# A matmul engine's order in a fused recommender kernel: the third and fourth group of transposes moved within the steady batch tiles

## The chip, the cores and the metric

The kernel runs on one core of one Trainium2 chip. The metric is the device time of one execution in microseconds (us). The kernel before takes 982.83 us, the median of three runs (972.28, 982.83 and 982.91).

Names used below: PE is TensorE (matmuls and transposes), ACT is ScalarE, DVE is VectorE, POOL is GpSimd, SP is SyncE. PEld stands for PE's weight loads.

## The reference, cut to what matters

```python
cont_emb = emb_table[:13][None, :, :] * conts[:, :, None]     # 2048 x 13 x 64
cate_emb = emb_table[cates]                                   # 2048 x 26 x 64, gathered
cc = concatenate([cont_emb, cate_emb], axis=1)                # 2048 x 39 x 64
gram = einsum('bfd,bgd->bfg', cc, cc)
pairs = gram[:, ROWS, COLS]                                   # 741 products of each sample
X = concatenate([cont_emb.reshape(B, -1), cate_emb.reshape(B, -1), pairs], axis=1)
X = relu(_layernorm(X @ W1 + b1, ln1_g, ln1_b))               # 3237 -> 1024
X = relu(_layernorm(X @ W2 + b2, ln2_g, ln2_b))               # 1024 -> 1024
logit = sigmoid(X @ Wout + bout)
```

## The kernel before, in words

The batch of 2048 samples is cut into 16 tiles of 128 samples. A first stage computes, tile by tile, the first layer's 1024 columns and stores them to DRAM; a second stage (from about 755 us on) reads them back and does the second layer. The change concerns the first stage alone.

A tile x of the first stage has these parts:

- POOL gathers 26 embedding columns into `xb`, one indirect DMA each (L488), in four groups of 8, 6, 6 and 6 (`GROUPS`, two columns to a k-tile). It runs one tile ahead: the gathers of group g of tile x+1 wait until PE has transposed group g of tile x. Within a tile some gathers wait further, by `progress`: the one numbered 7 for `f_hi`, 10 for `late_hi`, 14 for `ts_hi` of all four groups, and 21, 23 and 25 for the dots taken from PSUM.
- PE transposes each group (L547; "next 0" is group 0 of the next tile, "own 1", "own 2", "own 3" are the second, third and fourth group). ACT rounds the result into `x_hl` (L766), DVE makes the low part (L1061), and both copy it to the layouts that the gram products want: ACT at L772 (`g_still`) and L777 (`g_move`), DVE at L1068.
- PE makes the pairwise products in four pieces, "gram 0" to "gram 3" (L590). "gram 0" needs the copies of all four groups. ACT and DVE take each piece out of PSUM (L807, L808, L1146, L1147); gram 2 and gram 3 wait until the pieces 0 and 1 are taken.
- From these DVE makes the features; PE transposes them in two steps, "factor" (L561) and "late" (L568, L569), and ACT and DVE split them (L789 and L1126 for factor, L794, L1132, L799 and L1138 for late).
- The first layer is 19 k-tiles of six matmuls each (L523, L524, L525): 0 to 12 are the embeddings, 13 to 18 the features. k-tiles 13 to 18 of a tile are done one iteration later, with "factor prev" and "late prev". k-tile 16 waits for `tail_lo`, the end of the late features' split (L1138). Behind k-tile 18 DVE and ACT do the layer norm of that tile (L1164 to L1192, L822).

Each engine has an order of its own, written out by hand. PE's is a tuple: `FIRST` for tile 0, `SECOND` for tile 1, `STEADY` for tiles 2 to 14 (thirteen iterations, of which twelve stand in a loop that holds two), `LAST` for tile 15. The file defines `STEADY` twice, and the second definition holds. ACT's and DVE's order stands in their functions `iteration`. For ACT it is, behind the factor's split of tile x: two `g_move` copies, the third group's split of tile x+1, the late features' hi part, a `g_move` copy, the tail's hi part, a `g_move` copy, the fourth group's split, and then the copies of the third and fourth group. DVE has the third group's low part ahead of the late features' low part as well.

Of the kernel before, what the change touches and what calls it, by code (L numbers as in the profile page):

```python
# [80 lines left out]
V_TILES = (CONT + 1) // 2  # L81
V_FIRST = (V_TILES - 1, 0, 1, 2)
V_BEHIND = {3: 3, 6: 4, 9: 5}
V_LAST = 5
IN_FLIGHT = 4


STEADY = (0, "own 1", 1, 2, 3, "factor prev", 4, "own 2", "late prev", 13, 14, "own 3", 5, 15, 16, 17, 18, 6, 7,
          "gram 0", 8, "gram 1", 9, "gram 2", 10, "gram 3", 11, "next 0", 12)
FIRST = (V_TILES - 1, 0, 1, 2)  # L90
V_BEHIND = {3: 3, 6: 4, 9: 5}
V_LAST = 5
IN_FLIGHT = 4


STEADY = (0, "own 1", 1, 2, 3, "factor prev", 4, "late prev", 13, 14, 5, "own 2", 15, 16, 17, "own 3", 18, 6, 7,
          "gram 0", 8, "gram 1", 9, "gram 2", 10, "gram 3", 11, "next 0", 12)
FIRST = (0, 1, 2, 3, "own 1", 4, 5, 6, "v 4", "own 2", 7, 8, "v 5", "own 3", 9, 10, "gram 0", "gram 1", 11,
         "gram 2", "gram 3", "next 0", 12)
# [42 lines left out]
def build(nc, conts, cates, emb, W1, b1, g1, be1, W2, b2, g2, be2, Wout, bout, rows, out):  # L142
    h1_dram = nc.dram_tensor("h1_scratch", (P, TILES, HID), F32, kind="Internal").ap()

    with ExitStack() as memory:
# [244 lines left out]
        def v_rows(n):  # L390

            m = min(P, CONT * DIM - n * P)
            return raw_hi[EK + n][0:m, :] if n < NF else h1_row[0:m, :]
# [3 lines left out]
        def _(sp):  # L397
# [5 lines left out]
            for k in range(EK):  # L403
                loads.append((raw_lo[k][:, :], (CONT + 2 * k) * DIM, w1_in[k]))
                if k in V_BEHIND:
                    n = V_BEHIND[k]
                    loads.append((v_rows(n), n * P, v_rows_in[n]))
# [3 lines left out]
            for n, (to, row, landed) in enumerate(loads):  # L411
                if n >= IN_FLIGHT:
                    sp.wait_ge(loads[n - IN_FLIGHT][2], 16)
                sp.dma_start(to, W1[row:row + to.shape[0], :]).then_inc(landed, 16)
# [105 lines left out]
        def _(pe):  # L520
# [81 lines left out]
            def v_product(n):  # L602
# [3 lines left out]
                for h in range(2):  # L606
                    done = nc.tensor.matmul(acc[1][0:CONT, h, :], vbd[0:rows_n.shape[0], n, :],
                                            rows_n[:, h * HALF:(h + 1) * HALF],
                                            start=n == V_FIRST[0], stop=n == V_LAST)
                if n == V_LAST:  # L610
                    done.then_inc(v_done, 1)
# [41 lines left out]

            def iteration(x, par, order=STEADY, first=False, last=False):

                if not isinstance(x, int) or x >= 2:
                    pe.wait_ge(norm_act, x - 1)
                    pe.wait_ge(norm_dve, x - 1)
                elif x == 1:
                    pe.wait_ge(v_in, 1)  # L660
                for what in order:
                    if isinstance(what, str):
                        share(x, what, first, last)
                    elif what < EK:
                        if first:
                            pe.wait_ge(w1_split, what + 1)
                        done = k_tile(x, par, what)
                        if last:
                            done.then_inc(w1_free, 1)
                    else:  # L670
                        if isinstance(x, int) and x == 1:
                            pe.wait_ge(w1_split, what + 1)
                        k_tile(x - 1, 1 - par, what)
                if last:
                    for kt in range(EK, KT):
                        if kt == EK + 2:
                            late(x)
                            transpose2(0, 0)
                        done = k_tile(x, par, kt)
                        if kt < KT - 1:  # L680
                            done.then_inc(w1_free, 1)
                    product2(0, 0, first=True)
# [45 lines left out]

            iteration(0, 0, FIRST, first=True)
            iteration(1, 1, SECOND)  # L730
# [658 lines left out]
```

## Time and profile before

| | us |
|---|---|
| three runs, median (lowest to highest) | 982.83 (972.28 to 982.91) |
| the profiled execution, its own time | 965.06 |
| its span, first to last instruction | 963.0 |
| PE busy in the span | 798.1 (83%) |
| DVE, ACT, POOL busy | 554.5, 500.7, 486.3 |
| mean granted clock of PE, share of full speed | 0.92 |

Times of the trace count from the span's start. Matmuls are pipelined, so a row that lasts 0.39 us may start 0.23 us behind the row ahead of it; the step between starts is what a matmul costs. A gram 0 starts at 345.24, 390.96, 434.76 and so on; from one gram 0 to the next is called a period below. Thirteen iterations follow the order `STEADY`, and each ends with a gram 0, the first at 162.19 and the last at 705.27.

### The profile page before, as it was taken

What the parts mean: (1) busy time and instruction counts of PE and PEld (TensorE: products, weight loads), DVE (VectorE), ACT (ScalarE), POOL (GpSimd) and SP (SyncE); (2) the same over time, 40 slices, a digit from 0 to 9 for tenths busy, and PEclk for the clock granted to TensorE, in tenths of its full rate; (3) what the DMA queues carried; (4) which work ended last, traced back from release to release, by engine and by line L of the source; (5) the groups of instructions that cost most, each with busy time, mean ns of one, the idle gap of its engine ahead of it and who ended that gap; (6) DMA issues with size and microseconds to landing.
All of it is one profiled execution on the core that took longest, in us unless ns stands there. A gap on an engine that the chain in (4) does not pass through costs nothing.

```text
span 963.0 us, 11843 instructions
## 1 busy us (share of the span) xinstructions
PE 798.1 (83%) x3583; PEld 630.0 (65%) x3583; DVE 554.5 (58%) x1704; ACT 500.7 (52%) x878; POOL 486.3 (51%) x451
## 2 busy tenths in 40 slices
PE   5386878888888778878788888888889899999995
PEld 1255666667666666657566666666667788888884
DVE  6255645454647273757455554646377765666668
ACT  2285745454646364565545544646468654444441
POOL 6776555555556455656555555556550013333331
PEclk9797979888999889998998989899999999999998
DMA  9998233222223232323232322323234621111100
GB/s 246 140 166 100 18 39 41 20 39 21 38 20 42 17 41 18 43 17 43 17 43 17 41 24 35 40 19 41 20 41 152 216 69 44 44 44 44 44 0 1
DMA packets 26232, 50.69 MB, mean 53 GB/s; under 512 B 10413, under 2 KB 10669, under 8 KB 26208
## 3 DMA queue, kind: packets, MB, share of 16 engines
q0 software_dynamic: 13344, 13.71, 21.6%
q1 hardware_dynamic: 10128, 27.97, 9.2%
q10 hardware_dynamic: 2736, 8.71, 2.3%
q8 instruction: 12, 0.20, 0.1%
q14 instruction: 12, 0.10, 0.0%
HBM read 41.96 MB, written 8.40 MB: 52 GB/s over the span
## 4 chain that ended last, share of the span: by engine, by line
PE 53%; ACT 14%; issue 14%; DVE 9%; DMA 7%; another core or an unknown queue 3%; SPq 0%; ACTq 0%; DVEq 0%
PE acc L523 15%; PE acc L525 14%; PE acc L524 14%; ACT g_move L777 6%; DMA raw_lo<-in_L_rec_W 5%; PE gr L590 3%; PE tr L590 2%; ACT g_still L772 2%; PE tr L547 2%; ACT x_hl L766 2%; DVE dots L1146 2%; DMA raw_hi<-in_L_rec_W 1%; DVE g_still L1068 1%; ACT dots L807 1%
## 5 line engine op out<-in xcount | busy, mean ns | idle before, releaser
L488 POOL DMA_INDIRECT xb<-in_L_rec_emb_table,idx x416 | 417.5, 1003 | 298.0 <-issue 141.6
L523 PE MATMUL acc<-w_hi,x_hl 128*128 128x512 f32 x416 | 183.8, 442 | 22.3 <-issue 15.3
L525 PE MATMUL acc<-w_hi,x_hl 128*128 128x512 f32 x416 | 174.6, 420 | 0.0
L524 PE MATMUL acc<-w_lo,x_hl 128*128 128x512 f32 x416 | 174.2, 419 | 0.0
L777 ACT CAST g_move<-x_hl 64x384 fp32r<-64x384 f32 (+1 forms) x192 | 125.5, 654 | 2.8
L507 POOL TENSOR_TENSOR raw_lo<-raw_lo,raw_hi 128x1024 f32<-128x1024 f32 x14 | 33.5, 2396 | 160.5 <-ACT raw_lo L946 160.5
L523 PEld LDWEIGHTS acc<-w_hi,x_hl 128*128 128x128 f32 x416 | 85.3, 205 | 43.5 <-issue 20.2
L523 PE MATMUL acc<-w_hi 128*128 128x512 f32 x256 | 101.3, 396 | 1.6 <-DVE w_lo L1339 1.6
L523 PE MATMUL acc<-w_hi,f_slots 128*128 128x512 f32 x192 | 85.3, 444 | 19.7 <-DVE f_slots L1138 12.9
L772 ACT CAST g_still<-x_hl 64x384 fp32r<-64x384 f32 (+1 forms) x96 | 99.0, 1032 | 1.9
L525 PE MATMUL acc<-w_hi,w_lo 128*128 128x512 f32 x256 | 100.0, 390 | 0.0
L524 PE MATMUL acc<-w_lo,w_hi 128*128 128x512 f32 x256 | 99.6, 389 | 0.0
L525 PEld LDWEIGHTS acc<-w_hi,x_hl 128*128 128x128 f32 x416 | 85.2, 205 | 20.3
L524 PEld LDWEIGHTS acc<-w_lo,x_hl 128*128 128x128 f32 x416 | 85.7, 206 | 14.2
L1061 DVE TENSOR_TENSOR x_hl<-tr,x_hl 128x512 fp32r<-128x512 f32 (+1 forms) x32 | 20.0, 625 | 123.0 <-ACT x_hl L766 116.5
L590 PE MATMUL gr<-g_move,g_still 128*128 128x124 f32 x256 | 40.8, 318 | 52.1 <-ACT g_move L777 37.5
L1061 DVE TENSOR_TENSOR x_hl<-gr,x_hl 128x384 fp32r<-128x384 f32 x32 | 17.8, 557 | 108.1 <-issue 81.3
L524 PE MATMUL acc<-w_lo,f_slots 128*128 128x512 f32 x192 | 79.1, 412 | 0.0
L525 PE MATMUL acc<-w_hi,f_slots 128*128 128x512 f32 x192 | 78.8, 410 | 0.0
L590 PEld LDWEIGHTS gr<-g_move,g_still 128*128 128x128 f32 x256 | 37.2, 220 | 62.6 <-ACT g_move L777 41.8
L766 ACT CAST x_hl<-gr 128x384 fp32r<-128x384 f32 x32 | 15.4, 480 | 117.6 <-remote 55.1
L1068 DVE TENSOR_SCALAR g_still<-x_hl 64x384 fp32r<-64x384 f32 (+1 forms) x96 | 66.6, 694 | 1.9
(117 smaller groups left out, 1280.0 us busy)
## 6 DMA issues: line engine op xcount, KB each, us to landing
raw_lo<-in_L_rec_W SPq DMA_DIRECT2D x26, 512.0 KB, 4.6
h_scratch<-h_row ACTq DMA_DIRECT2D x16, 512.0 KB
raw_hi<-h_scratch SPq DMA_DIRECT2D x16, 512.0 KB, 3.6
xb<-in_L_rec_emb_table,idx POOLq DMA_INDIRECT x416
raw_hi<-in_L_rec_W SPq DMA_DIRECT2D x6, 512.0 KB, 5.3
raw_hi<-in_L_rec_b SPq DMA_DIRECT2D x1, 512.0 KB, 4.3
raw_hi<-in_L_rec_ln_g SPq DMA_DIRECT2D x1, 512.0 KB, 5.2
raw_hi<-in_L_rec_ln_b SPq DMA_DIRECT2D x1, 512.0 KB, 6.0
```

The source lines that it names most:

```text
L488: nc.gpsimd.indirect_dma_start(out=xb[:, f * DIM:(f + 1) * DIM], out_offset=None, in_=emb, in_offset=bass.IndirectOffsetOnAxis(ap=idx[:, p ...
L507: nc.gpsimd.tensor_tensor(a2[par][:, :], n2[par][:, :], g2_bc, ALU.mult).then_inc(a2_mul, 1)
L523: nc.tensor.matmul(o, a, w, start=first, stop=False)
L524: nc.tensor.matmul(o, a, v, start=False, stop=False)
L525: return nc.tensor.matmul(o, b, w, start=False, stop=last)
L547: last = nc.tensor.transpose(t_bank(g)[:, (kt - a) * P:(kt - a + 1) * P], xb[:, kt * P:(kt + 1) * P], ident[:, :])
L590: last = nc.tensor.matmul(to, g_still[:, SAMPLES * j:SAMPLES * (j + 1), :].rearrange("p s f -> p (s f)"), g_move[:, :, j:P:P // SAMPLES], ...
L766: nc.scalar.copy(x_hl[:, 0, a:b, :].rearrange("p k b -> p (k b)"), t_bank(g)[:, 0:n]).then_inc(ts_hi, 1)
L772: nc.scalar.copy(*still_part(0, n, of))
L777: last = nc.scalar.copy(*move_part(n, m // 2, m % 2))
L1061: TT(x_hl[:, 1, a:b, :].rearrange("p k b -> p (k b)"), t_bank(g)[:, 0:n], x_hl[:, 0, a:b, :].rearrange("p k b -> p (k b)").bitcast(F32), A ...
L1068: last = TS(to, x_lo.bitcast(F32), 2.0, None, ALU.mult)
```

## The change

The second definition of `STEADY` is taken out, together with the repeated lines around it, so that the first one holds. It differs in two places: "own 2" stands behind k-tile 4 and ahead of "late prev" (it stood behind k-tile 5), and "own 3" stands behind k-tile 14 (it stood behind k-tile 17). `FIRST`, `SECOND` and `LAST` stay, and so do the orders of ACT, DVE, POOL and SP.

```diff
 STEADY = (0, "own 1", 1, 2, 3, "factor prev", 4, "own 2", "late prev", 13, 14, "own 3", 5, 15, 16, 17, 18, 6, 7,
           "gram 0", 8, "gram 1", 9, "gram 2", 10, "gram 3", 11, "next 0", 12)
-FIRST = (V_TILES - 1, 0, 1, 2)
-V_BEHIND = {3: 3, 6: 4, 9: 5}
-V_LAST = 5
-IN_FLIGHT = 4
-
-
-STEADY = (0, "own 1", 1, 2, 3, "factor prev", 4, "late prev", 13, 14, 5, "own 2", 15, 16, 17, "own 3", 18, 6, 7,
-          "gram 0", 8, "gram 1", 9, "gram 2", 10, "gram 3", 11, "next 0", 12)
```

PE before, from the end of k-tile 4 to the fourth group's transposes (`acc0` takes this tile's k-tiles, `acc1` those of the tile before; `f_slots` are features, `xb` the gathered embeddings):

```order
L525 MATMUL acc0<-w1_hi,x_hl 128x512
L568 MATMUL gr<-ident,dots 128x128 [waits chosen_done]
...
L569 MATMUL gr<-ident,feats 59x128
L523 MATMUL acc1<-w1_hi,f_slots 128x512 [waits f_lo]
...
L547 MATMUL tr<-ident,xb 128x128 [waits ts_lo,gathered2]
...
L523 MATMUL acc1<-w1_hi,f_slots 128x512 [waits tail_lo]
...
L547 MATMUL gr<-ident,xb 128x128 [waits ts_lo,gathered3]
```

The same stretch of PE now (line numbers are eight lower):

```order
L517 MATMUL acc0<-w1_hi,x_hl 128x512
L539 MATMUL tr<-ident,xb 128x128 [waits ts_lo,gathered2]
...
L560 MATMUL gr<-ident,dots 128x128 [waits chosen_done]
...
L561 MATMUL gr<-ident,feats 59x128
L515 MATMUL acc1<-w1_hi,f_slots 128x512 [waits f_lo]
...
L539 MATMUL gr<-ident,xb 128x128 [waits ts_lo,gathered3]
...
L515 MATMUL acc1<-w1_hi,f_slots 128x512 [waits tail_lo]
```

The third group's transposes (`gathered2`) now stand ahead of the late features' transposes, and the fourth group's (`gathered3`) ahead of the k-tile that waits for `tail_lo` instead of behind it. Between the fourth group's transposes and gram 0 there are now seven k-tiles (5, 15, 16, 17, 18, 6, 7), before there were three (18, 6, 7).

ACT's order over the same work, which is not changed (`x_hl<-tr` and `x_hl<-gr` are the splits of the third and the fourth group):

```order
L789 CAST f_slots<-tr 128x384 [waits f_trans]
L777 COPY g_move<-x_hl 64x7x128 x2
...
L766 CAST x_hl<-tr 128x384 [waits trans_ready]
L794 CAST f_slots<-gr 128x384 [waits l_trans]
L777 COPY g_move<-x_hl 64x7x128
L799 CAST f_slots<-gr 59x128 [waits late_lo]
L777 COPY g_move<-x_hl 64x7x128
...
L766 CAST x_hl<-gr 128x384 [waits trans_ready]
```

PE's order now names the third group, the late features and the fourth group in the sequence in which ACT waits for them; before, the late features came first.

## Rows read from the trace of the kernel before

**Rows 1.** Who PE waited for, 140 to 710 us: total us, times, longest us.

```profile
PE gr L590 <- ACT g_move L777: 36.2, 10, 3.7
PE tr L561 <- issue: 19.6, 6, 4.3
PE acc L523 <- DVE f_slots L1138: 12.9, 13, 1.0
PE gr L568 <- remote: 11.2, 5, 2.3
PE gr L590 <- issue: 11.0, 3, 3.7
PE gr L568 <- DVE dots L1154: 3.9, 3, 1.6
```

**Rows 2.** Windows by period: us, busy by engine (x rows), granted clock, DMA share, GB/s.

```profile
162.19:705.27 543.08, 442.99 (x1992) 352.10 (x1993) 298.19 (x1032) 286.40 (x468) 309.45 (x312) 0.91 0.28 31
345.24:390.96 45.72, 37.64 (x166) 30.14 (x167) 25.08 (x87) 24.17 (x39) 25.84 (x26) 0.90 0.27 30
390.96:434.76 43.80, 36.51 (x166) 28.84 (x167) 24.83 (x87) 23.74 (x39) 25.77 (x27) 0.90 0.29 31
705.27:738.48 33.21, 32.79 (x161) 26.92 (x161) 24.88 (x86) 23.95 (x39) 7.60 (x9) 0.95 0.31 74
```

**Rows 3.** Timeline of PE: start us, us, engine, line, operation, tiles, [idle before <-releaser].

```profile
370.74 0.55 PE L568 MATMUL gr<-ident,dots 128*128 128x128 f32 x3 [2.21 <-remote]
...
376.96 0.49 PE L547 MATMUL tr<-ident,xb 128*128 128x128 f32 x3
...
379.84 0.50 PE L523 MATMUL acc<-w_hi,f_slots 128*128 128x512 f32 x1 [0.99 <-DVE f_slots L1138]
...
382.69 0.49 PE L547 MATMUL gr<-ident,xb 128*128 128x128 f32 x3
...
390.96 1.11 PE L590 MATMUL gr<-g_move,g_still 128*128 128x124 f32 x8 [3.67 <-issue]
```

**Rows 4.** Timeline of ACT, the same stretch.

```profile
369.06 1.89 ACT L777 CAST g_move<-x_hl 64x896 fp32r<-64x896 f32 x2
...
377.48 0.48 ACT L766 CAST x_hl<-tr 128x384 fp32r<-128x384 f32 x1 [6.54 <-PE tr L547]
...
383.22 0.48 ACT L766 CAST x_hl<-gr 128x384 fp32r<-128x384 f32 x1 [2.79 <-issue]
...
388.47 2.07 ACT L777 CAST g_move<-x_hl 64x384 fp32r<-64x384 f32 x4
```

**Rows 5.** Timeline of PE in the last tile, which follows `LAST`.

```profile
726.42 0.49 PE L547 MATMUL tr<-ident,xb 128*128 128x128 f32 x3
...
729.96 0.49 PE L547 MATMUL gr<-ident,xb 128*128 128x128 f32 x3
...
738.48 1.03 PE L590 MATMUL gr<-g_move,g_still 128*128 128x124 f32 x8
...
744.05 1.13 PE L590 MATMUL gr<-g_move,g_still 128*128 128x124 f32 x8 [0.85 <-ACT cc_dots L808]
```

**Rows 6.** Timeline of ACT in the last tile.

```profile
727.64 0.48 ACT L766 CAST x_hl<-tr 128x384 fp32r<-128x384 f32 x1
...
735.88 2.08 ACT L777 CAST g_move<-x_hl 64x384 fp32r<-64x384 f32 x4
```

**Rows 7.** Timeline, PE's transposes of a second group and ACT's split of them.

```profile
313.70 0.49 PE L547 MATMUL gr<-ident,xb 128*128 128x128 f32 x3
...
319.97 0.48 ACT L766 CAST x_hl<-gr 128x384 fp32r<-128x384 f32 x1 [8.54 <-remote]
```

**Rows 8.** Timeline of POOL and of DVE around three gathers.

```profile
384.32 2.46 DVE L1068 TENSOR_SCALAR g_still<-x_hl 64x896 fp32r<-64x896 f32 x2
...
384.80 2.11 POOL L488 DMA_INDIRECT xb<-in_L_rec_emb_table,idx  x1 [0.95 <-issue]
...
398.14 0.94 POOL L488 DMA_INDIRECT xb<-in_L_rec_emb_table,idx  x1 [3.72 <-ACT cc_dots L808]
399.39 0.94 POOL L488 DMA_INDIRECT xb<-in_L_rec_emb_table,idx  x1 [0.30 <-issue]
```

## Prediction

> **What bounds the kernel now.** Read the busy shares first: PE is busy for 83% of the span, every other engine for less than 60%. So the question is what PE waits for, and where. The list of PE's waits over the steady tiles [rows 1] has two things that the change touches. Gram 0 waits 3.7 us in each of thirteen iterations for ACT's last `g_move` copy: 36.2 and 11.0 us, the second part listed under "issue" with the same length. k-tile 16 waits 1.0 us thirteen times for L1138, the end of the late features: 12.9 us. The remaining waits, for factor (19.6) and late (11.2 and 3.9), are those that the change should leave.
>
> The windows by period come next [rows 2]: two steady periods take 45.72 and 43.80 us, and (705.27 − 162.19) / 12 = 45.3 us is the average, at a granted clock of 0.91. The last tile's period takes 33.21 us. It is the key row. Its order `LAST` has the third group behind k-tile 4 and the fourth behind 14, as the changed `STEADY` has. It also has one k-tile fewer between two grams, and no gathers beside it (POOL busy 7.6 us), so it is a precedent for the order and not for all of its surroundings.
>
> Then the timelines of one period show why gram 0 is late [rows 3, 4]. ACT ends its second pair of `g_move` copies at 369.06 + 1.89 = 370.95 and stands idle for 6.54 us, because its next instruction wants the third group's transposes, which PE does at 376.96. The late transposes are done at 371.4, but ACT's hi part of them stands behind that split. So the late features are ready only at 379.8 (k-tile 16 waits 0.99). ACT then idles 2.79 us until the fourth group's transposes at 382.69. From there to the end of its copies at 388.47 + 2.07 = 390.54 is 7.85 us, and PE has only three k-tiles (about 4.1 us) to cover it: gram 0 waits 3.67 us.
>
> **The change, term by term.** Nothing is added or removed: the same three transposes twice an iteration (0.25 us of PE each) stand elsewhere, in thirteen iterations.
>
> A k-tile at full clock: in the last tile the fourth group's transposes start at 729.96 and gram 0, six k-tiles later, at 738.48 [rows 5]. (8.52 − 0.25) / 6 = 1.38 us.
>
> Term 1, k-tile 16. ACT can split the third group as soon as it is free (370.95), then the late features (ready 371.4), then the tail, about 2.7 us in all with the copies between. I count with up to 3 us more for a signal that arrives late: 377. PE reaches k-tile 16 behind late (371.3), k-tiles 13 and 14 (376.96 − 371.3 less 1.38 for k-tile 5, 4.3 us), own 3, 5 and 15: 378.6 [rows 3]. The wait goes: 12.9 us.
>
> Term 2, gram 0. The fourth group's transposes end at about 375.8. ACT needs 8.0 us from their start to its last copy: in the last tile 729.96 to 735.88 + 2.08 = 737.96 [rows 5, 6]; with its backlog from late features about 9. PE now has 7 × 1.38 + 0.25 = 9.9 us of work in between. Cover is left over by 1 to 2 us, so all of the wait goes: 36.2 + 11.0 = 47.2 us. In the last tile the same chain with only six k-tiles of cover has gram 0 without any wait. If the cover were gone, each us that ACT ends later costs PE one.
>
> Term 3, the clock. The granted clock over the steady tiles is 0.91 of full speed, of 2.4 GHz; in single stretches it is 1.2 GHz. 0.09 × 543 = 49 us are lost so, 3.8 us a period. In the last period, which begins behind a gram 0 wait and has no other idle stretch of over 0.85 us, it is 0.95: 0.05 × 33.21 = 1.7 us. That is the price of one such wait. Without gram 0's wait 13 × 1.7 = 22 us come back. Bounds: nothing, if the waits that stay pull the clock down just as often, and 26 us if k-tile 16's wait contributed.
>
> Term 4, small things. The third group's transposes now stand ahead of late, whose wait (2.2 us in half of the iterations) hides them: 0.25 × 6 = 1.5 us. Against it, gram 2 may wait for ACT's taking of gram 0, since the layer norm ahead of it no longer starts so early against gram 0: 0.85 us in the last tile [rows 5], where one k-tile stands between gram 0 and gram 2 fewer cover it. With `STEADY`'s cover I take 0.15 × 13 = 2 us; bounds 0 and 0.85 × 13 = 11. Waits added on PE: own 2 wants gathers 14 to 19 and own 3 gathers 20 to 25; behind them everything on PE queues up. Gather 21 is issued at 398.14 [rows 8], so 25 goes out about 403, and its reader is the own 3 of the next iteration, one period behind the 375.8 of above, at about 415. More than 10 us of slack: costed at nothing. If that cover were gone, PE would idle one for one.
>
> POOL: its gathers 10 and 14 are freed by `late_hi` and by the fourth group's split, both now 3 to 7 us earlier. Its pauses shrink and it starts gather 21 sooner. It hides beside PE as long as its work a period stays under PE's: 26 gathers at 0.94 + 0.30 us [rows 8], one of them 1.8 us longer, is 34.0 us.
>
> Sum: 12.9 + 47.2 + 22 + 1.5 − 2 = 81.6 us. The profiled execution would go from 965.06 to about 883. A period would be 45.3 − 6.3 = 39.0 us. The precedent agrees: 33.2 + 1.4 for the extra k-tile + (19.6 + 11.2 + 3.9) / 13 = 2.7 for the waits that stay + up to 1.7 of clock is 37.3 to 39.0. The profiled execution lies 17.8 us under the median of the runs; I take the gain from the median: 982.83 − 81.6 = 901. A measurement of this kernel tells about 2% (20 us) from no change.
>
> **A rule of the skill against the change.** At 384.80 a gather takes 2.11 us and has 0.95 us ahead of it, against 0.94 and 0.30 elsewhere; DVE's L1068 copies run from 384.32 to 386.8 [rows 8]. The Trainium skill, SBUF — State Buffer (SBUF: two separate sides), says that a DMA issued by GpSimd is starved of descriptors while VectorE runs a two-port mode on fp32 in SBUF. By that rule, the trace agrees; and the change, which makes POOL's gathers run nearly without a pause, lets more of them meet such copies.
>
> **Rivals.**
>
> *A, the clock does not come back.* The waits at factor and late stay, and the clock may fall after them anyway. Then term 3 is gone: 901 + 22 = 923. For it: the clock is 0.90 even in the 43.80 us period [rows 2].
>
> *B, a held signal takes the place of the wait.* A signal can arrive long after its instruction: the second group's transposes end at 314.2, ACT starts on them at 319.97 [rows 7], 5.8 us later, while the next tile's first group is gathered. The third and fourth group are now transposed nearer to those gathers. Held by 5.8 us, the fourth group eats the 1.9 us of cover and leaves 3.9 us of wait at gram 0, with 1.7 us of clock: 5.6 us, in every second iteration 34 us: 935. In all of them it would be 974. Against it: the two splits at 377.48 and 383.22 start within 0.1 us of their transposes' end [rows 3, 4], with gathers about.
>
> *C, the other waits shrink too.* With POOL ahead of its time, gathers may no longer crowd behind next 0, and factor and late would run as in the last tile, without waits: 34.7 us and some clock go besides: 901 − 41 = 860. For it the last tile speaks, but that one has no gathers.
>
> *D, slower: POOL becomes the bound.* Each gather that meets DVE's copies costs POOL 1.8 us more (1.17 longer, 0.65 more gap). POOL stands at 34.0 us a period; 2.8 more held gathers reach my 39.0, and from (45.3 − 34.0) / 1.8 = 6.3 more on, the kernel is slower than before. With eight more it is 48.4 us a period, 13 × 3.1 = 40 us above: 1023. Against it: the longest stretch of DVE's L1068 copies in a period is 2.46 us [rows 8], room for about two gathers.
>
> **Chances.** The forecast (901, its own range 885 to 918) 0.45; A 0.2; B 0.17; C 0.14; D 0.04. Less than 963 is faster by over 2%: all of the forecast, A and C, and most of B (0.13), 0.92. Same 0.05: B in most iterations, and part of D. Slower 0.03. The range reaches from C to B: 862 to 942.
>
> **What would show it.** Right: no wait of L523 for L1138 and none of L590 for L777 in the steady tiles; ACT's split of the third group starts straight behind its copies; periods of 38 to 40 us; a granted clock above 0.93. Term 3 is wrong if the clock stays at 0.91. B shows as ACT idle ahead of a fourth group's split that PE finished microseconds earlier; C as shorter waits at L561 and L568; D as POOL without a pause and PE waiting for gathered columns at L547. The forecast as a whole is wrong if a period stays above 42 us.

## The result, and the profile after

The kernel after takes 934.62 us (median of 6 runs, 932.81 to 940.31), the kernel before beside it 973.61 us (968.07 to 982.91). The ratio is 0.9623, 95% interval 0.9593 to 0.9653: faster, by 36.7 us (the medians themselves differ by 39.0). Ratios compare the fast executions of two kernels run side by side, so they can differ a little from the ratio of the medians. The forecast was right in sign and inside its range, and its size, 81.6 us, was over twice what came. The profiled execution went from 965.06 to 936.18 us, its span from 963.0 to 934.1.

The page of the kernel after, its busy shares:

```profile
PE 787.4 (84%) x3583; PEld 626.4 (67%) x3583; DVE 555.2 (59%) x1704; ACT 501.4 (54%) x878; POOL 489.2 (52%) x451
```

The windows of the kernel after (stretch, its length, busy time of PE, PEld, DVE, ACT and POOL with their instructions, granted clock, DMA share, GB/s): twelve steady periods, and the last tile's.

```profile
159.09:672.42 513.33, 436.07 (x1993) 351.04 (x1992) 298.86 (x1032) 286.98 (x468) 312.74 (x312) 0.91 0.33 32
672.42:709.62 37.20, 32.82 (x161) 26.90 (x160) 23.77 (x85) 23.95 (x39) 9.46 (x10) 0.95 0.34 68
```

A steady period is 513.33 / 12 = 42.8 us, where it was 45.3 and 39.0 was forecast. By the prediction's own last sign, a period above 42 us, the forecast as a whole was wrong. The clock stands at 0.91, as before [rows 2].

PE's waits of the kernel after, steady tiles (us in total, times, longest us):

```profile
PE tr L582 <- DVE cc_dots L1139: 20.0, 6, 3.5
PE gr L582 <- DVE cc_dots L1139: 11.8, 7, 4.6
PE gr L560 <- remote: 10.0, 5, 2.1
PE gr L560 <- DVE dots L1146: 9.1, 7, 1.9
PE gr L582 <- issue: 7.9, 8, 1.4
PE acc L515 <- issue: 6.0, 4, 1.7
PE acc L517 <- issue: 4.5, 6, 1.0
```

Beside [rows 1]: the two waits that the change was to remove are gone, k-tile 16's and gram 0's for `g_move` (gram 0 still waits 0.6 to 0.8 us in four of thirteen iterations). Factor's wait of 19.6 us is gone too. In their place stand waits at L582 for `cc_dots` (L1139). That is gram 2 and gram 3 waiting until the pieces 0 and 1 are taken from PSUM.

A split of the period shows it. Taken from the starts in the PE timelines, iterations 3 to 14, the mean stretch from next 0 to gram 0 fell from 33.19 to 26.13 us, and the stretch from gram 0 to next 0 rose from 12.06 to 16.65. Over twelve periods that is 85 us won and 55 us given back. The next timeline has one such stretch, of four engines (start, duration, engine and line, [idle before it and what ended it]):

```profile
460.10 1.03 PE L582 MATMUL gr<-g_move,g_still 128*128 128x124 f32 x8
...
462.38 1.03 PE L582 MATMUL tr<-g_move,g_still 128*128 128x124 f32 x8
462.44 0.20 ACT L805 ACTIVATE st<-st 128x1 f32<-128x1 f32 x1 [3.49 <-DVE st L1162]
462.67 0.16 DVE L1164 RECIPROCAL st<-st 128x1 f32<-128x1 f32 x1 [0.27 <-issue]
...
463.78 0.78 ACT L814 ACTIVATE h_row<-acc,st 128x512 f32<-128x512 f32 x1 [1.14 <-DVE st L1172]
...
464.99 0.94 POOL L480 DMA_INDIRECT xb<-in_L_rec_emb_table,idx  x1 [0.30 <-issue]
...
466.94 0.39 PE L515 MATMUL acc<-w_hi,x_hl 128*128 128x512 f32 x1 [1.72 <-issue]
467.83 1.05 ACT L799 ACTIVATE dots<-gr 32x208 f32<-32x208 f32 x2 [3.27 <-remote]
467.83 1.05 DVE L1138 TENSOR_SCALAR dots<-gr 32x208 f32<-32x208 f32 x2 [3.41 <-remote]
...
469.47 1.94 PE L582 MATMUL gr<-g_move,g_still 128*128 128x124 f32 x8 [0.77 <-DVE cc_dots L1139]
```

Gram 0 ends at 461.1 and gram 1 at 463.4. ACT and DVE have done the layer norm and are free at 464.6. Both start taking gram 0 at 467.83, in the same instant, after more than 3 us with nothing to do. The trace records the updates of the semaphore that they wait for. The first two behind gram 0 are recorded at 467.81 and 467.95; taken in order they are gram 0's and gram 1's, 6.7 and 4.5 us behind the matmuls. I call such a signal held. POOL's last gather before it ended at 465.93. Not every signal is held: at 462.44 to 462.67, in the same run of gathers, ACT and DVE answer each other at once. The waits of the two engines show how often it happens:

```profile
DVE dots L1138 <- remote: 58.0, 13, 5.3
ACT dots L799 <- remote: 51.9, 13, 4.5
```

ACT and DVE stand in front of a piece for 4.0 and 4.5 us in every iteration, and PE behind them. There are two kinds of iteration. In seven of thirteen gram 0's signal is held and gram 2 waits: above it starts at 469.47, 9.37 us behind gram 0 (8.7 to 9.4 in all seven; 4.7 in e1 below). In the other six gram 0's comes at once, gram 1's is held, and gram 3 waits. Here gram 1 had ended at 421.22:

```profile
428.35 1.03 ACT L799 ACTIVATE dots<-tr 32x208 f32<-32x208 f32 x2 [4.41 <-remote]
...
429.97 1.94 PE L582 MATMUL tr<-g_move,g_still 128*128 128x124 f32 x8 [3.42 <-DVE cc_dots L1139]
```

POOL's timeline tells the two kinds apart, and both from the kernel before. Call gathers with less than 0.8 us between them a run. In the kernel before, gram 0 ends within a run of 7 gathers in all thirteen iterations (384.80 to 394.42 in [rows 8]'s). In the kernel after it is a run of 14 in the seven iterations of the first kind, and of 11 in the six of the second. The first gather of a run of 14 (number 7, which waits for `f_hi`), and, from the kernel before, the last of a run of 7 and DVE's taking of gram 0 behind it:

```profile
447.50 0.94 POOL L480 DMA_INDIRECT xb<-in_L_rec_emb_table,idx  x1 [2.81 <-ACT f_slots L781]
```

```profile
393.47 0.95 POOL L488 DMA_INDIRECT xb<-in_L_rec_emb_table,idx  x1 [0.30 <-issue]
...
394.80 1.05 DVE L1146 TENSOR_SCALAR dots<-gr 32x208 f32<-32x208 f32 x2
```

The run of 7 begins with gather 14, which waits for the fourth group's split. The change makes that split earlier, and the late features' as well, for which gather 10 waits. So POOL no longer pauses ahead of gather 14, and in half of the iterations not ahead of gather 10 either. In the kernel before gram 0's and gram 1's signals are not held: where their updates are recorded (7 and 13 of 13) they are at most 0.03 us behind the matmuls, and DVE takes gram 0 directly behind its layer norm.

### The profile page after: what moved, and what is told of

Its sections match the earlier page's. It is cut to its first block, busy times and chain, and to the rows that moved or that the text cites. A ratio compares the mean times of both kernels' runs of the same rounds, so it can differ in the third digit from the quotient of the medians.

```text
span 934.1 us, 11843 instructions
## 1 busy us (share of the span) xinstructions
PE 787.4 (84%) x3583; PEld 626.4 (67%) x3583; DVE 555.2 (59%) x1704; ACT 501.4 (54%) x878; POOL 489.2 (52%) x451
## 4 chain that ended last, share of the span: by engine, by line
PE 39%; ACT 17%; DVE 16%; another core or an unknown queue 14%; issue 11%; DMA 2%; SPq 0%; ACTq 0%; DVEq 0%
PE acc L515 11%; PE acc L516 10%; PE acc L517 10%; ACT g_move L769 7%; DVE g_still L1060 5%; ACT g_still L764 4%; DVE dots L1138 3%; PE tr L582 2%; ACT x_hl L758 2%; DMA raw_lo<-in_L_rec_W 2%; DVE feats L1087 2%; DVE small L1156 2%; PE gr L582 1%; DVE cc_dots L1139 1%
## 5 line engine op out<-in xcount | busy, mean ns | idle before, releaser
L769 ACT CAST g_move<-x_hl 64x384 fp32r<-64x384 f32 (+1 forms) x192 | 125.7, 655 | 2.8
L499 POOL TENSOR_TENSOR raw_lo<-raw_lo,raw_hi 128x1024 f32<-128x1024 f32 x14 | 33.5, 2394 | 162.1 <-ACT raw_lo L938 162.1
L515 PE MATMUL acc<-w_hi,f_slots 128*128 128x512 f32 x192 | 78.0, 406 | 7.8 <-DVE f_slots L1118 4.5
L517 PE MATMUL acc<-w_hi,f_slots 128*128 128x512 f32 x192 | 76.3, 397 | 0.0
L516 PE MATMUL acc<-w_lo,f_slots 128*128 128x512 f32 x192 | 76.3, 397 | 0.0
L1281 DVE TENSOR_TENSOR w_lo<-raw_lo,w_hi 128x256 fp32r<-128x256 f32 x64 | 34.5, 553 | 51.5 <-ACT w_hi L930 51.4
L582 PE MATMUL gr<-g_move,g_still 128*128 128x124 f32 x256 | 39.7, 314 | 29.8 <-DVE cc_dots L1139 17.7
L1138 DVE TENSOR_SCALAR dots<-tr 32x208 f32<-32x208 f32 x64 | 33.1, 518 | 51.7 <-remote 31.0
L582 PEld LDWEIGHTS gr<-g_move,g_still 128*128 128x128 f32 x256 | 36.4, 215 | 40.8 <-ACT cc_dots L800 22.4
```

The lines of the kernel that those rows point to most:

```text
L499: nc.gpsimd.tensor_tensor(a2[par][:, :], n2[par][:, :], g2_bc, ALU.mult).then_inc(a2_mul, 1)
L515: nc.tensor.matmul(o, a, w, start=first, stop=False)
L516: nc.tensor.matmul(o, a, v, start=False, stop=False)
L517: return nc.tensor.matmul(o, b, w, start=False, stop=last)
L582: last = nc.tensor.matmul(to, g_still[:, SAMPLES * j:SAMPLES * (j + 1), :].rearrange("p s f -> p (s f)"), g_move[:, :, j:P:P // SAMPLES], ...
L769: last = nc.scalar.copy(*move_part(n, m // 2, m % 2))
```

## The experiments

In the expectations, theory H is that the time given back is held signals and that POOL's gathers hold them; N is that it is the layer norm's chain on ACT and DVE between gram 0 and its taking; P is that POOL's issuing of indirect gathers does it, and not the transfers. The kernel before was run beside each group of experiments: 976.17 us for e1 to e4, 970.35 for e5 to e8, 898.59 for e9 to e11 and 897.22 for e12, each the median of 7. The last two numbers are a finding of their own.

### Without gathers: e1 and e2

The kernel after (e1) and before (e2), with POOL's gathers of tiles 2 to 15 and PE's waits for them left out, so that these tiles are computed on tile 1's columns.

```diff
-            with pool.Fori(0, (TILES - 2) // 2) as i:
-                for u in range(2):
-                    gather(2 * i + (2 + u), u, tied=True)
...
-                pe.wait_ge(gathered[g], n * x + n)
+                if isinstance(x, int) and x < 2:
+                    pe.wait_ge(gathered[g], n * x + n)
```

> The changed order with the gathers of tiles 2 to 15 left out (POOL does not issue them and PE does not wait for them; the tiles are computed from tile 1's columns). Theory H, held signals: the changed kernel lost 4.3 us a period between gram 0 and next 0 (11.9 us before, 16.2 now) because the signal of gram 0 or gram 1 reaches ACT and DVE some 4.4 us late when a run of gathers ends just ahead of it. Without gathers no signal is held: gram 0 to next 0 takes 10 to 10.5 us, a period 33.5 to 35 us, the kernel 820 to 840 us. Theory N, the norm chain: the stretch is long because the layer norm on DVE and ACT ends only 4 us behind gram 0, gathers or not: gram 0 to next 0 stays at 15 us or more, a period at 38 or more, the kernel at 875 or more.

> The order of before with the same gathers left out. Theory H: the waits that the prediction priced, 3.7 us at gram 0 and 1.0 us at k-tile 16, do not depend on gathers and stay in all thirteen iterations, while factor, late and the second group lose their waits: a period of about 40 us, the kernel 900 to 915 us, so that the change without gathers would be worth 70 to 85 us, the 82 us that were forecast. Theory N: the change is worth without gathers what it is with them, 30 to 40 us.

Measured: e1 800.18 us (ratio to before 0.8249, 0.8146 to 0.8353); e2 902.11 (0.9281, 0.9181 to 0.9381). Without gathers the change is worth 101.9 us, more than the 70 to 85 expected. The layer norm's chain is unchanged, and gram 0 to next 0 takes 9.9 us in e1, where N had 15 or more: N falls and H stands, though e1 is 20 us below the range that H gave. No signal is recorded more than 0.3 us behind its instruction in either. PE's waits of e2, and under them those of e1, each over its steady tiles:

```profile
PE gr L588 <- ACT g_move L775: 45.9, 13, 3.6
PE acc L520 <- DVE f_slots L1136: 12.9, 13, 1.0
PE tr L545 <- DVE cc_dots L1145: 3.9, 12, 0.3
```

```profile
PE tr L537 <- DVE cc_dots L1137: 3.8, 12, 0.3
PE gr L580 <- ACT cc_dots L798: 0.6, 2, 0.3
```

and a steady window of each, e2 first:

```profile
148.00:640.00 492.00, 433.23 (x1996) 350.72 (x1997) 296.46 (x1034) 288.56 (x469) 0.00 (x0) 0.92 0.03 13
```

```profile
138.42:541.00 402.58, 397.52 (x2024) 325.55 (x2023) 300.85 (x1053) 290.66 (x475) 0.00 (x0) 1.00 0.04 16
```

Here the forecast's terms can be read one by one. Terms 1 and 2 are e2's 45.9 + 12.9 = 58.8 us; forecast 60.1. Term 3 is PE's busy time per instruction, 433.23 / 1996 = 0.2171 us against 397.52 / 2024 = 0.1964; times 166 instructions a period and 13 periods it is 45 us, where 22 was forecast with a bound of 26. The sum, 103 us, is what was measured (102).

### Each half alone: e3 and e4

e3 moves the third group alone and leaves "own 3" behind k-tile 17. e4 moves the fourth group alone, directly behind "own 2", which stays behind k-tile 5. Against the kernel after, e3's line first:

```diff
-STEADY = (0, "own 1", 1, 2, 3, "factor prev", 4, "own 2", "late prev", 13, 14, "own 3", 5, 15, 16, 17, 18, 6, 7,
+STEADY = (0, "own 1", 1, 2, 3, "factor prev", 4, "own 2", "late prev", 13, 14, 5, 15, 16, 17, "own 3", 18, 6, 7,
```

```diff
-STEADY = (0, "own 1", 1, 2, 3, "factor prev", 4, "own 2", "late prev", 13, 14, "own 3", 5, 15, 16, 17, 18, 6, 7,
+STEADY = (0, "own 1", 1, 2, 3, "factor prev", 4, "late prev", 13, 14, 5, "own 2", "own 3", 15, 16, 17, 18, 6, 7,
```

> Only the third group moved (behind k-tile 4); the fourth stays behind k-tile 17. Both theories: the 1.0 us at k-tile 16 goes (13 us), the wait at gram 0 stays near 3.7 us, since the chain from the fourth group's transposes to the last copy and its three k-tiles of cover are as before. 955 to 962 us against 974 of before. If the gain of the whole change came from the third group, it would be 935 to 945.

> The third group stays behind k-tile 5, the fourth is moved up right behind it (three k-tiles earlier than before). ACT splits it behind the late features, at about 10 us ahead of gram 0; PE has 15, 16, 17, 18, 6, 7 in between. The wait at k-tile 16 stays (1.0 us), the wait at gram 0 falls from 3.7 to about 1.4 us. Theory H: the time won at gram 0 is given back in part behind it, at gram 1 or gram 2, as in the changed kernel: 945 to 960 us. Theory N: the same order of size, 945 to 955.

Measured: e3 955.78 us (0.9861, 0.9755 to 0.9966), e4 960.27 (0.989, 0.9783 to 0.9996): by the ratios 14 and 11 us, each within some 10 us, so neither is by itself clear of 2%. Together they are 24 us; whether the halves add up to the 36.7 us of the whole stays open. e3 keeps a wait of gram 0 for `g_move` (`PE gr L582 <- ACT g_move L769: 37.8, 9, 5.0` between 160 and 690 us) and has gram 0 to next 0 at 13.3 us. In e4 gram 0's wait is down to about 1.2 us in each iteration (1.4 were expected), and it has 16.0 us from gram 0 to next 0. POOL's runs go with it. In e3 gram 0 ends within a run of 7 gathers in all thirteen iterations, as in the kernel before, and neither gram 0's nor gram 1's signal is held. In e4 it is a run of 11 or 13, and gram 1's signal is held in all thirteen, by 4.2 to 7.2 us. So what removes most of gram 0's wait, the fourth group's move, also takes POOL's pause ahead of gather 14 away, and the signals are held behind it.

### What holds the signals: e5, e6, e8

e5 puts the same number of copies in the place of POOL's gathers, under the same waits, from SP and without indices; it reads the table's first 128 rows every time. e6 leaves out every second gather of tiles 2 to 15. e8 gathers everything, and has one pause a tile instead of six.

Their edits, in this order:

```diff
+                        for f in range(2 * a, 2 * b):
+                            progress(x, f)
+                            sp.dma_start(xb[:, f * DIM:(f + 1) * DIM], emb[0:P, :]).then_inc(copied[g], 16)
```

```diff
                             progress(x, f)
+                            if f % 2:
+                                continue
```

```diff
-                if f == 7:
-                    pool.wait_ge(f_hi, x - 1)
...
-                elif f in (21, 23, 25):
-                    pool.wait_ge(taken_act, FILLS * (x - 1) + (f - 19) // 2)
...
+                if f == 14:
+                    pool.wait_ge(taken_act, FILLS * (x - 1) + 1)
+                    stands_alone(pool)
```

> The changed order; for tiles 2 to 15 POOL's indirect gathers are left out, and SP issues as many plain copies of the same size (128 rows of 256 bytes each, always the first 128 rows of the table) into the same columns, under the same waits. It asks what of a gather holds the signals. Theory T, the transfers: 26 small DMAs a tile and their landings hold the signals whoever issues them; gram 0 to next 0 stays near 16 us, the kernel at 900 us or more. Theory P, POOL's part: it is the software gather (its descriptors written by POOL) that holds them; gram 0 to next 0 is about 10 us and the kernel 800 to 825 us, as without gathers.

> The changed order; in tiles 2 to 15 every second column is not gathered (13 gathers a tile instead of 26, in the same places, runs half as long). If signals are held only when a run of gathers has piled up a backlog, holds nearly vanish: gram 0 to next 0 10 to 11.5 us, the kernel 800 to 830 us. If each gather holds signals for itself, half of the loss stays: about 13 us, the kernel 860 to 880 us.

> The changed order; POOL's waits ahead of gathers 7, 10, 14, 21, 23 and 25 are replaced by one ahead of gather 14, for the taking of gram 0. Gathers 0 to 13 run behind next 0 in one go, then POOL is quiet until gram 0 is taken, then 14 to 25. Theory H: gram 0's signal is not held and gram 0 to next 0 takes 10 to 12 us, but the longer runs hold factor, late and the group splits more: next 0 to gram 0 26 to 30 us. Kernel 890 to 940 us; the sum tells whether pacing can give the lost time back.

Measured: e5 802.52 us (796.15 to 809.01), e6 801.39 (0.8286, 0.8218 to 0.8354), both at the 800.18 of e1; in neither does an engine stand ahead of a signal that is held. So transfers of that number and size cost the engines nothing, which speaks for P, and half the gathers cost nothing as well. e5 changes the issuer, the queue and the scattered rows together, so it does not tell which of these it is. e8 missed its expectation by 200 us: 1137.66 us (1.1741, 1.166 to 1.1822). Its first half came as H said: with no gather near gram 0, gram 0 to next 0 is 9.8 us. But next 0 to gram 0 is 48.3. Its long runs are the clearest case of a held signal. Its timeline (POOL's first and last gather of one run of 26, the factor transposes, and who waits for them):

```profile
409.34 0.95 POOL L471 DMA_INDIRECT xb<-in_L_rec_emb_table,idx  x1 [25.31 <-issue]
...
440.71 0.95 POOL L471 DMA_INDIRECT xb<-in_L_rec_emb_table,idx  x1 [0.30 <-issue]
```

```profile
426.10 0.90 PE L544 MATMUL tr<-ident,feats 128*128 128x128 f32 x3 [4.51 <-issue]
...
445.90 0.90 PE L551 MATMUL gr<-ident,dots 128*128 128x128 f32 x3 [15.70 <-remote]
446.02 0.48 ACT L772 CAST f_slots<-tr 128x384 fp32r<-128x384 f32 x1 [18.57 <-remote]
```

```profile
437.44 0.16 DVE L1137 TENSOR_TENSOR dots<-h_row 128x2 f32<-128x2 f32 x1 [0.54 <-issue]
438.84 0.16 DVE L1137 TENSOR_TENSOR dots<-h_row 128x1 f32<-128x1 f32 x1 [1.24 <-issue]
```

The factor transposes end at 427.0; ACT, idle for 18.57 us, starts on them at 446.02, 4.4 us behind the end of POOL's last gather (441.65). PE's late transposes (L551) are let go at 445.90, by a signal of DVE, at nearly the same time. In this condition a signal that falls into a long run of gathers can be held until the run has ended, and in a run of 26 that is up to 19 us.

Held signals are not the whole of it. DVE's additions of L1137 (the last two lines) wait for no semaphore, and DVE stops for 0.5 to 1.2 us ahead of each of the last ten. In the kernel after, PE stops in the same way in the middle of k-tiles (466.94 above; 12.5 us in twelve periods). Between 150 and 530 us no run without held signals (e1, e2, e5, e6, e9, e11) has such a stop of over 0.3 us on PE or DVE. So what the gathers do reaches instructions that need no signal; no run here shows how.

### A pause elsewhere: e7

```diff
-                elif f in (21, 23, 25):
-                    pool.wait_ge(taken_act, FILLS * (x - 1) + (f - 19) // 2)
+                elif f in (17, 23, 25):
+                    pool.wait_ge(taken_act, FILLS * (x - 1) + (f - 15) // 2 if f == 17 else FILLS * (x - 1) + (f - 19) // 2)
```

> The changed order; POOL's wait for the taking of gram 0 stands ahead of gather 17 instead of gather 21, nothing left out. The run of gathers ahead of gram 0 is four shorter and ends some 5 us earlier. Theory H: the signals of gram 0 and gram 1 are held less, gram 0 to next 0 falls from 16.7 to 12 to 14 us; the four gathers come later and lengthen the run into next 0, so that factor and late may wait longer. Kernel 905 to 930 us against 935 for the change. Were the place of the gathers without weight, it would be 935 within 5.

Measured: 950.91 us (0.9821, 0.972 to 0.9923), a miss of H's range and worse than the kernel after (0.9623). The pause does what it is for: POOL's run, now of 10, ends ahead of gram 0, gram 0's and gram 1's signals are held by 0.9 us at most, and gram 0 to next 0 falls from 16.7 to 10.6 us. But the gathers that no longer stand there make a run of 16 behind it, and the held signals stand there. PE's waits of e7, steady tiles:

```profile
PE tr L553 <- issue: 53.6, 8, 8.6
PE gr L560 <- DVE dots L1146: 16.1, 5, 4.4
PE tr L553 <- DVE feats L1111: 13.0, 4, 4.4
```

Factor (L553) waits up to 8.6 us, and next 0 to gram 0 rises from 26.1 to 33.2. Pauses choose which signal is held; they don't make it free.

### The same gathers, nothing held: e9 to e12

e9 puts k-tile 10 ahead of gram 2, to cover its wait. e10 leaves out every fourth gather. e11 has all gathers, and cuts POOL's longest run. e12 is e9 once more. The edits of e9, e10 and e11:

```diff
-           "gram 0", 8, "gram 1", 9, "gram 2", 10, "gram 3", 11, "next 0", 12)
+           "gram 0", 8, "gram 1", 9, 10, "gram 2", 11, "gram 3", "next 0", 12)
```

```diff
+                            if f % 4 == 3:
+                                continue
```

```diff
                 elif f == 14:
-                    pool.wait_ge(ts_hi, NG * x)
+                    pool.wait_ge(tail_lo, x - 1)
+                elif f == 17:
+                    pool.wait_ge(xg_hi, XN * x)
```

> The kernel after, with k-tile 10 ahead of gram 2 and gram 3 directly ahead of next 0 with k-tile 11 between gram 2 and gram 3. Theory H (what the change gives back is gram 2's wait for a taking of gram 0 whose ready signal is held 3 to 4.4 us): 1.4 us more of matmuls stand over that wait, so a period gets up to 1.4 us shorter: 918 to 930 us, and the stretch from gram 0 to next 0 without a wait stays above 16. If the time that is given back is not in that wait but anywhere else (rival: PE's stalls in the middle of k-tiles, the late features), nothing changes: 932 to 940.

> The kernel after with every fourth embedding column of tiles 2 to 15 not gathered (20 gathers a tile for 26), so it computes on old columns there. Theory of a threshold (a signal is held once POOL's gathers follow each other too long): near 802 us, as with half the gathers, or at most 840. Theory of a share (held time goes with the number of gathers): 802 plus half of the 133 us between it and the kernel after, 865 us.

> The kernel after with all 26 gathers, but its longest run cut: gather 14 waits for the late features' low part of the tail, gather 17 for the copies of all groups, so that runs of 4, 3 and 4 stand where one of 11 or 14 stood. If the length of a run is what holds signals: gram 0's signal is held under 2 us and the time is 900 to 925 us. If only the number of gathers per period counts: 930 to 950, with the held time moved to other signals.

> The same kernel as e9 (k-tile 10 ahead of gram 2), once more, since in the call of e9 the kernel before itself took 898.6 us and no signal was held. If the kernel before takes about 970 us this time and signals are held: with the time given back in gram 2's wait, 918 to 930 us; with it elsewhere, 932 to 940. If the kernel before takes about 898 us again: 805 to 815 us, as in e9, and the two conditions belong to the chips or to their state, not to the kernels.

Measured: e9 809.83 us (0.8998, 0.8936 to 0.9061), e10 795.59 (0.887, 0.8805 to 0.8936), e11 802.88 (0.8924, 0.8872 to 0.8976), e12 810.91 (0.9057, 0.8977 to 0.9136). e9 and e11 are far below what either theory expected; e10 has the time of its theory of a threshold and e12 that of its last case (805 to 815). The times must not be read alone: the kernel before, unchanged, took 898.59 and 897.22 us beside them, not 970. It ran there as e2 did, which has no gathers. The groups ran on different chips of the same type: e1 to e4 on one, e5 to e8 on a second, e9 to e11 on a third and e12 on a fourth. On the third and fourth no signal is held in any trace, with all 26 gathers a tile; in e9 POOL runs through five periods without a pause of 0.8 us. So e10 tests no threshold. A window of e11 over its twelve steady periods, and PE's waits for gathers in it:

```profile
138.42:541.00 402.58, 392.51 (x1993) 320.05 (x1992) 297.74 (x1033) 287.49 (x468) 308.68 (x309) 1.00 0.66 41
```

```profile
PE gr L542 <- DMA xb<-in_L_rec_emb_table,idx: 3.8, 4, 1.6
```

A period is 402.58 / 12 = 33.5 us at a clock of 1.00. So e11's order, which is the kernel after's on PE, ACT and DVE, is worth 898.59 - 802.88 = 95.7 us there. The kernel after itself was not run in this condition; e11 differs from it in POOL's waits alone. Since no signal is held, e11's cut runs and e9's cover had nothing to act on. e9's order costs 7 us against e11 (34.2 us a period for 33.5): gram 3 now stands directly ahead of next 0, which waits for its taking by 1.66 us each time. Whether e9 or e11 would beat the kernel after where signals are held stays open; both groups that were to tell ran where none are.

One more difference between the conditions is in the profile's list of DMA issues. The kernel after, then e11 (the last figure is the median time to landing, us):

```profile
xb<-in_L_rec_emb_table,idx POOLq DMA_INDIRECT x416
```

```profile
xb<-in_L_rec_emb_table,idx POOLq DMA_INDIRECT x416, 6.2
```

For the kernel after no landing time can be given, since the semaphore updates of the gathers are recorded incompletely: 835 of 2048 for the first group, against 2042 in e11. The engines' own updates have gaps too: those of the gram pieces' semaphore are 52 of 64 in the kernel after, 64 of 64 in e11. Of e5's copies all are recorded, on a chip of the first condition. But the gaps are no mark of a held signal: e1 has 145 of 256 updates of the first group and e6 741 of 1152, on the chips of the first condition, with nothing held. They go with the chip or its state. The experiments tell what holds signals within that condition (POOL's indirect gathers, close together). They don't tell what makes a chip, or an hour, one or the other: something of the DMA path, or the recording itself. Every time here comes with a record, so this rival, that the kernel is slowed only while it is recorded, is not excluded by any run. Two groups fell into each condition, and by their times the runs of before and after that the result rests on into the first.

## Why the prediction was right and wrong

**Terms 1 and 2** (60.1 us) were right but for 2.8 us that gram 0 still waits. The waits of k-tile 16 and gram 0 are gone in the kernel after, and e2 has them at 58.8 us where nothing else disturbs.

**Term 4** was mis-sized, and this is the step that failed: "gram 2 may wait for ACT's taking of gram 0", at 2 us with a bound of 11. It measured +4.6 us a period from gram 0 to next 0, 55 us over twelve, in waits at gram 2 and gram 3 (11.8 and 20.0 us), in stalls of PE in the middle of k-tiles (466.94: 1.72 us of "issue") and in the low clock behind them. Behind it stands the paragraph on POOL. It says that the pauses ahead of gathers 10 and 14 shrink, and prices that at nothing as long as POOL's work fits into a period. That the shorter pauses join runs of 7 gathers into runs of 11 and 14 around gram 0 was not seen. I took term 4 from the last tile, whose one gram 2 waits 0.85 us, and had noted that this tile has no gathers beside it. That was the very thing to price: [rows 7] shows a signal held by 5.8 us, in a steady tile with gathers.

**Term 3**, the clock, was wrong in both directions. Where signals are held it is 0.91 as before; PE's busy time per instruction fell from 0.2224 us (442.99 / 1992, [rows 2]) to 0.2188 (436.07 / 1993), 8 us in all. The new waits pull it down as the old ones did: behind the wait ahead of 469.47 a matmul takes 0.43 us from start to start, ahead of gram 0 it took 0.23. Where none are held it rises from 0.92 to 1.00 and gives 45 us, twice the term and above its bound of 26: I had priced one wait from a stretch at 0.95 which still contained low clock of its own, instead of letting the whole loss of 49 us be the upper end.

**The rivals.** A (the clock does not come back) is what happened to term 3, but for 8 us. B had the right mechanism in the wrong place: it held the fourth group's transposes and had gram 0 pay. Its 935 us, beside the 934.62 measured, is luck, and the range was met because it reached down to B. Signals of transposes are held in the kernel after as well (ACT's split of the third group starts 2.03 us late at 491.21, behind transposes that PE began at 486.46), and no gram 0 waits for `g_move` because of it. The signals that cost are gram 0's and gram 1's own, with two k-tiles and one other piece between each of them and the piece that waits. The order before kept them out of long runs of gathers; that is why its trace had no row of it. C came in part: factor's 19.6 us is gone, while late's waits are 19.1 us (10.0 + 9.1) against 15.1 before. D did not come: POOL keeps up. But e11 shows how near it is: 26 gathers at 1.25 us are 32.5 us, its period is 33.5, and PE's first waits for gathers are there. On such a chip the next gain has to come from POOL's work as well.

**The account.** Of the 85 us won between next 0 and gram 0 in twelve periods, some 55 are terms 1 and 2 (60 in thirteen), and 30 are factor's wait (19.6) and a little clock, which the forecast left out. Less 55 given back it is 30; the span fell by 28.9. Against e1 and e2, the gathers, with held signals and stops together, cost the kernel before 45.26 - 40.92 = 4.3 us a period and the kernel after 42.78 - 33.05 = 9.7 us. The difference, 5.4 x 13 = 70 us, is what separates the 102 us of the change alone from the 36.7 measured (65). The cited rule, that VectorE's two-port modes starve a DMA issued by GpSimd of descriptors (the Trainium skill, SBUF — State Buffer (SBUF: two separate sides)), concerned POOL's own pace. Gathers of over 1.5 us are 13 among 242 in the kernel after and 8 among 227 in the kernel before, between 160 and 560 us, and each of them meets DVE's copies into `g_still`. The trace agrees in kind, and it decided nothing.

## What to carry to other kernels

When a precedent is taken from the same trace, list what does not run beside it, and price that from the nearest row that has it; here it was one row, read and then used for the wrong place. When a wait is removed, the work behind it starts earlier, and every signal it needs is then needed earlier. Ask as well which pauses of the other engines it shortens, and what then runs beside the signals that PE needs next; match each recorded update to its own instruction, since some are not recorded. Run the kernel before beside every experiment, on the same chip: 78 us of difference between two groups of runs of the same kernel would have passed for the gain of e9 or e11.

## What was not expected of the hardware

- On two of the chips, with POOL's indirect gathers close together, semaphore signals of PE arrive up to 7 us late, and 19 us late in a run of 26 (e8); PE and DVE also stop ahead of instructions that wait for nothing. Other signals in the same run come at once. Half the gathers (13 a tile), or the same number of plain copies from SP, hold none (e6, e5).
- This depends on the chip, its state or the recording: the same kernel takes 976 and 970 us on two chips, and 899 and 897 on two others, where no signal is held with all gathers.
- The granted clock goes from 0.92 to 1.00 over a whole stage when waits of 3.5 and 1.0 us a period are taken out (e2 and e1), worth 45 of 102 us.
